# A sixteen-layer hybrid block on one core: the first phase runs layer by layer over both pairs of a stream, and the filter of the state space layer is prepared later

## The reference

```
x = x + mamba(norm(x));            x = x + experts(norm(x))
x = x + linear_attention(norm(x)); x = x + experts(norm(x))        # same weights again
x = x + windowed_attention(norm(x)); x = x + channel_mix(norm(x))
x = x + delta_rule(norm(x));       x = x + channel_mix(norm(x))    # same weights again
x = x + state_space(norm(x))       # a causal filter of 256 taps for each of 256 channels
... 7 more sublayers (low-rank linear, attention, gated deep network) ...
```

## Time and profile before

| | us |
|---|---|
| runs | 2987.4, 2991.18, 2996.92 |
| median | 2991.18 |
| span of the profiled execution, first to last instruction | 2973.9 |
| median of the runs less that span | 17.3 |
| busy: PE, DVE, ACT, POOL | 2455.8, 2084.7, 1434.7, 560.2 |
| end of phase one in the trace (B's last addition into x) | 2016.6 |
| first matmul of the state space's filter | 2041.5 |

### The profile page before, as it was taken

One profiled execution on the slowest core, in us unless ns is written; L12 is line 12 of the kernel. 1 busy time (PEld: TensorE's weight loads), 2 busy tenths in 40 slices (PEclk: granted clock), 3 DMA queues, 4 the chain that ended last, 5 costly groups with the idle time before them and its releaser, 6 DMA issues. The chain is left out here.

```text
span 2973.9 us, 42131 instructions
## 1 busy us (share of the span) xinstructions
PE 2455.8 (83%) x16214; PEld 1563.1 (53%) x16214; DVE 2084.7 (70%) x4048; ACT 1434.7 (48%) x2603; POOL 560.2 (19%) x482
## 2 busy tenths in 40 slices
PE   5789897886797677897978869967778989789889
PEld 1257574454586322675744546835555554555554
DVE  6988887998998999998879976575572142652331
ACT  5533335884652365333358866445234434335342
POOL 2710001224792037000012205600010100000100
PEclk8999998998887679999979989978889999899999
DMA  3000000110000000000021110002000000000000
GB/s 156 0 1 1 1 1 24 42 43 12 1 1 1 0 1 0 1 28 8 1 85 42 43 62 11 2 0 52 29 1 1 1 2 1 8 1 1 1 2 7
DMA packets 28888, 49.96 MB, mean 17 GB/s; under 512 B 5264, under 2 KB 18320, under 8 KB 28176
## 3 DMA queue, kind: packets, MB, share of 16 engines
q1 hardware_dynamic: 26384, 45.17, 5.0%
q10 hardware_dynamic: 2304, 2.10, 0.3%
HBM read 26.94 MB, written 1.44 MB: 10 GB/s over the span
## 5 line engine op out<-in xcount | busy, mean ns | idle before, releaser
L146 PEld LDWEIGHTS ps<-held_ffn,hidden 128*128 128x128 f32 x2304 | 301.0, 192 | 142.4 <-issue 122.7
L164 ACT ACTIVATE grown<-ps,bias_grown 128x512 f32<-128x512 f32 x288 | 197.9, 687 | 310.5 <-PE ps L146 310.5
L146 PE MATMUL ps<-held_ffn,hidden 128*128 128x128 f32 x2304 | 305.2, 276 | 9.8 <-DVE hidden L183 9.8
L177 POOL TENSOR_TENSOR qk<-conv,held_const 128x512 f32<-128x512 f32 x64 | 89.7, 1402 | 944.4 <-DVE conv L183 944.4
L183 DVE SCALAR_TENSOR_TENSOR conv<-conv_in,held_l1a,conv 128x512 f32<-128x512 f32 x288 | 235.6, 838 | 18.7 <-ACT conv L164 15.9
L177 POOL TENSOR_TENSOR long<-long,product 128x512 f32<-128x512 f32 x136 | 198.3, 1511 | 124.5 <-ACT product L164 122.8
L183 DVE SCALAR_TENSOR_TENSOR hidden<-ps,bias_kept,grown 128x512 f32<-128x512 f32 x288 | 215.0, 748 | 7.3
L180 DVE TENSOR_SCALAR grown<-grown,bias_fallen 128x512 f32<-128x512 f32 x288 | 138.5, 481 | 59.5 <-ACT grown L164 53.2
L177 POOL TENSOR_TENSOR part<-state,c_rows 128x512 f32<-128x512 f32 x128 | 162.8, 1297 | 81.5 <-issue 34.7
L207 POOL MEMSET wide_q<- 128x1536 f32 x8 | 11.0, 1378 | 833.2 <-DVE stream_b L180 783.4
L146 PE MATMUL ps<-part,held_const 128*128 128x512 f32 x256 | 147.3, 674 | 6.9 <-POOL part L177 4.6
(11 more groups left out here) (456 smaller groups left out, 5477.5 us busy)
## 6 DMA issues: line engine op xcount, KB each, us to landing
turned<-conv SPq DMA_DIRECT2D x256, 64.0 KB, 2.0
ring<-lags SPq DMA_DIRECT2D x64, 128.0 KB
held_ffn<-in_ffn SPq DMA_DIRECT2D x1, 4690.0 KB, 17.9
held_l1a<-in_l1a SPq DMA_DIRECT2D x2, 2120.0 KB, 15.5
held_l3f<-in_l3f SPq DMA_DIRECT2D x1, 2824.0 KB, 12.2
yT<-y ACTq DMA_DIRECT2D x16, 128.0 KB, 4.9
out<-x SPq DMA_DIRECT2D x4, 256.0 KB, 2.6
held_rows<-in_rows SPq DMA_DIRECT2D x1, 788.5 KB, 7.2
```

The costliest lines, as they stand in the source:

```text
L146: ins = self.real.matmul(out, lhsT, rhs, **kw)
L164: return self.sent(self.real.activation(out, a, func, **kw), 0.13 + columns(out) / 1150, 0.14)
L177: return self.vector(self.real.tensor_tensor(out, a, b, op), columns(out), out, a, b)
```

## The change

Each stream runs each layer for its first pair and then for its second pair, before the next layer. The layers and their operations are the same, 2595 ACT instructions with 89 table loads before and after among them. Counts of finished layers that others wait for are set anew: the filter's memory is free after the 10th layer of each stream (both sliding attentions) and the experts' memory after the 8th. The scheduler's catching up covers the 10th to 12th layer, not the 8th to 10th. The second load of `l1a` is gone.

```diff
@@ windowed_attention
-    st.windowed += 1
-    loaded = 16 * st.windowed
+    loaded = 16
@@ constants
+WINDOWS_DONE = 10
+EXPERTS_DONE = 8
@@ build
-    m.weave.catch_up = range(8, 11)
+    m.weave.catch_up = range(10, 13)
-    m.ring_free = [(st.x_done, len(PHASE_ONE) + 5) for st in streams]
-    ffn_free = [(st.x_done, len(PHASE_ONE) + 4) for st in streams]
+    m.ring_free = [(st.x_done, WINDOWS_DONE) for st in streams]
+    ffn_free = [(st.x_done, EXPERTS_DONE) for st in streams]
-        layers[st.name] = [layer(m, st, x(k)) for k in pairs for layer in PHASE_ONE]
-    three = [(x(1), 1, (B.x_done, len(PHASE_ONE))), (x(0), 0, None), (x(2), 2, None)]
+        layers[st.name] = [layer(m, st, x(k)) for layer in PHASE_ONE for k in pairs]
+    three = [(x(1), 1, (B.x_done, 2 * len(PHASE_ONE) - 1)), (x(0), 0, None), (x(2), 2, None)]
@@ filter_loads
-        for st in streams:
-            yield sp.wait_ge(st.x_done, 5)
+        for free in m.ring_free:
+            yield sp.wait_ge(*free)
         sp.dma_start(held["l2p"][:, :], m.a["l2p"]).then_inc(m.load["l2p"], 16)
-        yield sp.wait_ge(m.filter_stored, 48)
-        sp.dma_start(held["l1a"][:, :], m.a["l1a"]).then_inc(m.load["l1a"], 16)
```

More of the change, by code:

```diff
@@ L2723, in build @@
     m.weave.finished = {1: A.x_done.times, 2: B.x_done.times}
-    m.weave.catch_up = range(8, 11)
+    m.weave.catch_up = range(10, 13)
     for st in streams:
-        st.windowed = 0
         st.turns, st.turned, st.x_in = [Signal(f"{st.name}_turn_{r}") for r in range(2)], 0, x_in
```

## The result

| | before | after |
|---|---|---|
| median of 20 runs each, us | 2994.86 | 3004.89 |
| lowest and highest | 2972.31, 3008.57 | 2997.89, 3017.3 |
| profiled execution: span | 2973.9 | 3000.6 |

The changed kernel takes 1.0035 of the time before, 95% interval 1.0018 to 1.0052: some 10 us slower. The time lay in the predicted range; the direction did not come out as forecast.

What follows compares the result with a forecast made beforehand. Phase one was taken as bound by DVE or PE depending on the layer, with neither full in the delta rule's last part. -7 + 12 - 7 = -2 gave a span of 2972, plus 17.3 a time of 2989, range 2966 to 3012.

Steps and rivals of the forecast that it cites:

- Term 1, the filter: Phase one: the filter's DVE work, moved among the layers, would cost 85 us instead of 92: -7, bounds -15 to +13.
- Term 2, the end of phase one: Phase one's end: B leads by about 22, so the recurrence starts 41 behind the middle, not 29.4: +12, bounds +5 to +17.
- Term 3, streams apart: Delta rules: one stream's triangle beside the other's head or last part fills PE better: -7, between 0 and -15.
- A layer costs what it cost: Phase one's layers: same operations, both streams at the same kind of layer at nearly the same time, so 0.
- Nothing behind `spread` changes: From the first `spread` on, every engine's order is unchanged; only what precedes the recurrence can move, unless waits change: 0.
- The removed load: SP's queue: dropping the second load of `l1a`, which stands far ahead of the transfers needing it, gives 0, at most 15.5 us.
- the windows: The filter's windows (`ring<-lags`) wait for a filter ending in the second delta rule's triangle, well ahead of the recurrence: 0.
- The first one: Second delta rule: the filter's 38 us find no room and cost all their time, +20 on the sum, 3009; chance 0.22.
- The rival that ended faster: Delta rules: the lead pays more than it costs, -15 to -18, and the filter -8 more, 2972; chance 0.23.

Runs made afterwards that it cites:

- before_b_ahead_at_end: Kernel before, with the stretch that puts stream B's work ahead moved from layers 9 to 11 to layers 14 to 16; 3017.15 us, ratio 1.0080.
- after_b_ahead_late: Changed kernel with stream B's work put ahead in layers 14 to 16, not 11 to 13; 2996.26 us, 1.0012 of the time before.
- after_level_end: Changed kernel without the stretch that puts B's work ahead, also called the level kernel; 2987.89 us, 0.9983 of the time before, 0.9975 when repeated.
- before_level_end: Kernel before, without its own stretch (layers 9 to 11) that puts stream B's work ahead; 2995.34 us, 0.9990 of the time before.
- level_no_filter: after_level_end with the filter's preparation (112 VectorE operations) left out; 2920.07 us, 0.9739 of the time before.
- after_first_pairwise: Changed kernel with first five, then last three layers pair by pair, filter behind the second sliding attention, nothing put ahead for B; 3021.0 us, 1.0088.

## Why the prediction was off, by its steps

**Term 1, the filter (−7).** With nothing put ahead the filter costs 72 us (mean of 0.9983 and 0.9975, less 0.9739) against 75 before: −3, in the direction of the term and inside what the intervals allow. In the changed kernel itself, with its lead, it costs 75 and 87: 0 to +12, outside the forecast's −7. Part of that is the delta rules' loss under term 3, so the two can't be added. The 92 us for before were 75. The pairs of stretches from one execution had differences of the granted clock in them (triangles at 0.91 and 1.00), and the last delta rule, read as 242, was 251 in the second profile; how much of the 17 us is due to that is not shown. Both delta rules together were forecast at 298 + 260 = 558 and took 557 and 567; with the streams in step it is 547, since 26 us of filter work, and in another kernel 41, cost nothing that can be seen in the second one. `product<-back,ahead` took 1744 ns in the median in the second triangle, where POOL was busy for 37.4 of 42 us, and 1215 in the experts, where it was idle. At 8 operations that is 4 us of DVE's time. The Trainium skill, SBUF — State Buffer, section "SBUF: two separate sides", says that a VectorE operation with two SBUF inputs and a GpSimd operation that reads SBUF exclude each other; the trace agrees in direction.

**Term 2, the end of phase one (+12).** Right in place, mechanism and size: B's lead was 22.3 (forecast 22), A's end to the recurrence 31.6 (about 30), the recurrence 42.75 behind the middle (41), so +13.3. `before_b_ahead_at_end` shows the same (+10.7) in the old order, and `after_b_ahead_late` in the new one (39.0 against 28.8).

**Term 3, streams apart (−7): the step that failed, in its sign.** I had read that PE is nearly full in the triangle and DVE in the head, and argued that a stream's triangle beside the other's head fills both. The runs show no such gain. With filter work in it, the second delta rule takes 249 to 251 when its streams go in 2 to 8 us apart, 257 at 17 when A then overtakes, 271 (two profiles) at 17 when B stays ahead, and 279 at 21 when A stays ahead. Without filter work, B's lead in the last delta rule of `before_b_ahead_at_end` went with 263 against 259. Both delta rules together are 9 to 20 us longer in the changed kernel than in the level one. So the term was −7 and measured +9 to +20, outside the bounds of 0 to −15, which I had drawn on one side of zero only, without a row that excluded a loss. That the lead also moves 19 us of the filter's work from the first delta rule into the second was in no term either.

**"A layer costs what it cost" (0).** Right for the time, by the kernels without filter and without lead (0.9739, 0.9751). In detail a channel mix beside another one in step is dearer: level, the two last ones take 34.3 from the delta rules' ends, in the changed kernel 29.55, and one alone 15 before. The experts stayed at 135 to 137 (forecast 134 to 136).

**Nothing behind `spread` changes (0).** The recurrence's start to the end took 938.9 and 935.2 after, 932.4 and 932.2 before. So there are 3 to 7 us more, whose cause no run here settles: `before_b_ahead_at_end`, whose order there is that of the kernel before, took 944.0. In variants in which the scheduler also wrote another order for phase two it was 935.5 (`after_level_end`) to 951.0.

**The removed load (0), the windows (0).** The one load landed in 22.2 us. PE's waits for `ring` were 19.6 us, against 18.0 and 17.5 before.

**The rivals.** The first one (the filter finds no room in the second delta rule, 3009) is nearest in time, but its mechanism is not what happened: up to 41 us of filter work found room for nothing. The long second delta rules are those with a lead that stays. The rival that ended faster had the lead pay; it costs. As measured, from the level kernel, which is 6 us below the one before (0.9979): +14 at the recurrence, +9 to +20 in the delta rules, −5 in the last channel mixes (29.55 against 34.3), together +12 to +23 against before. The two measurements were +10 and +23.

## What to carry to other kernels

If two streams share the engines and a serial stage follows, ask which stream's last step is the longest chain to that stage and let it end first; a later end of that stream delays the serial stage by as much (here it starts 31.6 us after A's end when A is last, 24 after B's when B is last). Do not count on streams that are apart to fill the engines better: here background work hid in a stage while the foreground streams were in step, and the stage was some 20 us longer where they stayed 17 or more apart. Before a difference between two kernels is called the price of something, look in both traces whether it is there at all: here the kernel without the filter had the setting but not the lead. When a reordering also moves a scheduler's setting, time each by itself: here one number cost 16 to 30 us and hid the few that the order may have brought.

## What the runs showed of the hardware

- One kernel's executions spread by 36 us (2972.31 to 3008.57), and stretches with them: its second delta rule took 242.0 and 251.5 us in two profiles, and 258.7 in `before_level_end`, at granted clocks of 0.90, 0.84 and 0.85. In `level_no_filter` 253 us went with a granted clock of 0.85, and 239 with 0.90:
```profile
1422.00:1675.00 253.00, 206.06 (x1340) 153.39 (x1340) 160.07 (x329) 135.40 (x226) 83.96 (x68) 0.85 0.03 12
1675.00:1914.00 239.00, 193.60 (x1344) 149.74 (x1343) 158.84 (x332) 131.52 (x221) 83.94 (x68) 0.90 0.00 1
```
  A term of less than 10 us for such a stretch can't be read from a single profile here.
- PE's busy time in the second delta rule grows from 205 us (`after_level_end`) to 216 (the changed kernel) and 227 (`after_first_pairwise`), where the streams are apart, with nearly the same number of matmuls (1343 to 1353). The granted clock goes from 0.86 to 0.85 in the first step, which by itself would give 208, and to 0.82 in the second, which would give 215. Why each matmul is longer there stays open.
